# A look-ahead of three steps instead of six for the row maxima of a causal attention

## The reference

```python
h = layernorm(x) * (1 + ca) + sa
q = h @ wq            # 32 heads of 8
k, v = h @ wk, h @ wv # 8 heads of 8, each shared by 4 query heads
att = q @ k.T / sqrt(8), causal mask
att = softmax(att)    # over 1024 keys
x = x + ga * ((att @ v) @ wo)
h = layernorm(x) * (1 + cb) + sb
x = x + gb * ffn(h)   # 16 experts, top 4, and a shared one
```

## Time and profile before

| | |
|---|---|
| median of 3 runs | 1020.0 us (1019.06 to 1022.02) |
| profiled execution: its own time, its span | 1020.0 us, 1018.3 us |
| attention stage: first unit to first score | 89.7 to 124.28 us |
| attention stage: first score to the last product's end | 124.28 to about 603.9 us |
| TensorE busy over the span | 936.2 us (92%) |
| VectorE, ScalarE, GpSimd busy | 696.2, 434.4, 203.1 us |

### The profile page before, as it was taken

The page is one execution under the profiler, slowest core; times in us unless marked ns, Lnnn a source line. Parts: engine busy times, 40 slices in busy tenths (PEclk is TensorE's granted clock), DMA queues, the critical chain, the costliest instruction groups (busy, mean ns, idle before and its releaser), DMA issues. The chain is left out here.

```text
span 1018.3 us, 15458 instructions
## 1 busy us (share of the span) xinstructions
PE 936.2 (92%) x5728; PEld 687.0 (67%) x5728; DVE 696.2 (68%) x1242; ACT 434.4 (43%) x624; POOL 203.1 (20%) x241
## 2 busy tenths in 40 slices
PE   2884999999999999999999977769999999999996
PEld 2643766666666666666666426757888888888885
DVE  6535978877778877778877315478666666665665
ACT  1010066666666656566656761412232232223221
POOL 9500022221111211111211212487000000000000
PEclk8695599999999999999999998579999999999998
DMA  5174003333112222112220015143000000000000
GB/s 171 57 149 139 18 14 72 70 61 56 35 36 57 54 46 56 34 37 56 52 48 16 23 60 158 31 124 95 1 13 8 0 0 21 0 0 21 0 0 21
DMA packets 40550, 48.60 MB, mean 48 GB/s; under 512 B 10000, under 2 KB 29456, under 8 KB 39952
## 3 DMA queue, kind: packets, MB, share of 16 engines
q1 hardware_dynamic: 40496, 47.88, 19.8%
HBM read 29.77 MB, written 17.56 MB: 46 GB/s over the span
## 5 line engine op out<-in xcount | busy, mean ns | idle before, releaser
L574 ACT ACTIVATE probs<-psum 128x1024 f32<-128x1024 f32 (+3 forms) x384 | 294.5, 812 | 204.1 <-PE psum L624 202.3
L675 DVE TENSOR_REDUCE max_parts<-psum 128x1 f32<-128x512 f32 (+2 forms) x384 | 257.0, 687 | 13.4 <-PE psum L611 7.6
L624 PE MATMUL psum<-qs,ks 128*128 128x512 f32 (+3 forms) x768 | 208.3, 355 | 1.1 <-ACT probs L574 0.6
L671 DVE TENSOR_REDUCE max_parts<-psum 128x1 f32<-128x512 f32 x192 | 132.5, 690 | 78.3 <-PE psum L598 75.6
L638 PE MATMUL psum<-probs,v_aug 128*32 128x512 f32 (+3 forms) x1536 | 163.4, 498 | 0.2 <-POOL probs L551 0.2
L948 ACT ACTIVATE mid<-psum 128x512 f32<-128x512 f32 x80 | 47.9, 599 | 243.4 <-PE psum L971 243.4
L624 PEld LDWEIGHTS psum<-qs,ks 128*128 128x128 f32 x768 | 131.1, 189 | 25.9 <-ACT probs L574 15.8
L551 POOL TENSOR_SCALAR_AFFINE_SELECT probs<-probs 128x512 f32<-128x512 f32 x128 | 81.4, 636 | 300.9 <-ACT probs L574 300.9
L608 PE MATMUL psum<-ks,qs 128*128 128x256 f32 (+3 forms) x448 | 134.7, 335 | 0.0
L1059 DVE TENSOR_TENSOR mid<-mid,psum 128x512 f32<-128x512 f32 x80 | 54.9, 687 | 104.0 <-ACT mid L948 103.4
L611 PE MATMUL psum<-kd,qs 128*128 128x128 f32 x512 | 101.3, 267 | 18.3 <-DVE ks L691 18.3
(11 more groups left out here) (127 smaller groups left out, 1002.9 us busy)
## 6 DMA issues: line engine op xcount, KB each, us to landing
qs<-q_parts SPq DMA_DIRECT2D x32, 256.0 KB
y_sums<-y_sb SPq DMA_DIRECT2D x32, 256.0 KB, 2.3
wl_raw<-in_L_ffn_we_dram SPq DMA_DIRECT2D x36, 128.0 KB, 2.3
x_sb<-in_L_attn_x_dram SPq DMA_DIRECT2D x4, 512.0 KB, 7.2
q_parts<-w_hi SPq DMA_DIRECT2D x8, 256.0 KB
k_parts<-k_parts_sb SPq DMA_DIRECT2D x16, 128.0 KB
q_parts<-w_lo SPq DMA_DIRECT2D x8, 256.0 KB
ks<-k_parts SPq DMA_DIRECT2D x16, 128.0 KB
```

The costliest lines, as they stand in the source:

```text
L574: act.activation(probs[:, s % (LAG + 1), 2 * hh:2 * hh + 2, off:TT], psum[:, 2 * hh:2 * hh + 2, off:TT], ACT.Exp, scale=SCALE).then_inc(p_ ...
L624: last = pe.matmul(bank[2 * hh + hp][:, off:TT], ks[buf][:, c * P:(c + 1) * P], qs[buf][:, 2 * hh + hp, half * TT + off:(half + 1) * TT], ...
L671: dve.tensor_reduce(out=max_parts[:, hh, hp, i:i + 1, 1], in_=bank[unit_bank[u % 3]][:], axis=AX.X, op=ALU.max).then_inc(unit_free, 1)
L675: dve.tensor_reduce(out=max_parts[:, h0:h1, kind, slice(*tiles), slot], in_=bank[unit_bank[u % 3]].rearrange("p (s w) -> p s w", w=w), axi ...
```

## The change

The look-ahead becomes three triples, and the place of `split_rows` on GpSimd moves from behind s7's to behind s9's mask, because the last triple of the next group now falls in s8 instead of s5. TensorE, VectorE and SyncE take their new order from the constant; no instruction is added or removed over the whole kernel.

```diff
-AHEAD = 6
+AHEAD = 3
...
-                        if s == NSTEP - AHEAD + 1 and group + 1 < GROUPS:
+                        if s == NSTEP - AHEAD and group + 1 < GROUPS:
                             split_rows(group + 1)
```

## The result

The changed kernel takes 1075.62 us (median of 4, 1073.38 to 1081.94), the kernel before 1021.01 us (median of 4). The ratio is 1.0545, 95% interval 1.0495 to 1.0595. The direction was right and the size wrong: +13 us was forecast, up to +22 in the range, and +55 us came. The span grew from 1018.3 to 1075.2 us, by 56.9.

A forecast was written before the change was run, and what follows sets the result against it. TensorE was taken to bound the attention stage, so added waits cost one for one. Start -4.4, moved units +2.2, boundary waits +12.0 and last boundary +3.2 gave +13.0 us on 1020.0: 1033 us, range 1020 to 1042.

The forecast's parts named there:

- The start: Attention stage's first score: at 119.9 instead of 124.28 us, gaining 4.4 us; up to 1.5 us of low clock allowed.
- The moved units and the stream: Nine units moved into s6 to s8 of group 14 cost 2.2 us; a group's TensorE stream stays 30.73 us.
- the stream would get shorter: Rival, 8%: heavy triples beside the shortest scores shorten each group by over 0.87 us; at 1.1 us, 1016.5 us total.
- The chain to the read: Group boundary, from s9's first score (t9): cast at t9 + 3.0, first write t9 + 3.57, read issued t9 + 6.40.
- The slow chains: Writes-to-read chains at 14 boundaries: five exceed 2.83 us, by 4.6 us together, passing through as waits.
- the forecast's own lower bound: Low end of the forecast's own bounds, 1024 to 1042 us, before the range took in most of the just-in-time case.
- Before group 15: Last boundary, where s9 to s11 have no units: TensorE waits 3.2 us (2.7 to 3.7).
- the landing of the read: Read of the rows of maxima: lands 2.0 us after issue (1.5 to 2.5), at t9 + 8.40, so TensorE waits 0.53 us.
- the score that was due later: Next group's first score at a boundary: due 7.87 us after s9's first score (t9).
- the falling clock: Rival, 8%: after a wait, above all before group 15, TensorE falls to 1.2 GHz, costing 5 to 6 us; 1039 total.
- the rows come just in time: Rival, 14%: read lands in 1.5 us, writes no slower than 2.83, no wait at 14 boundaries; 1020 us, within 0.3%.
- the forecast's mechanism: Main case, 70%: TensorE waits for the rows of maxima at each group boundary; 1025 to 1042 us.

The follow-up runs named there:

- e2: Changed kernel with GpSimd's split of the rows behind s8's mask instead of s9's: 1036.41 us, ratio 1.0145 to the kernel before.
- e1: Changed kernel with SyncE sending the five loads of load_stacks after the sums of the group before, not right behind the rows' read: 1049.71 us, ratio 1.0288.
- e3: Changed kernel with eight extra overwritten matmuls of 512 columns ahead of the wait for the rows, from group 1 on: 1058.83 us, ratio 1.0375.
- e9: Kernel before with the split behind s9's mask and eight overwritten matmuls ahead of the wait for the rows: 1073.83 us, ratio 1.0524.
- e4: Kernel before, look-ahead of six kept, with only the split moved behind s9's mask: 1090.48 us, ratio 1.0685.

## Why the prediction was wrong

**The start: right.** First score at 120.24 (forecast 119.9), after a wait of 1.16 us (0.6). The clock rose 2.9 us behind it, at 123.1, instead of 0.9 us behind it, at 125.2; that costs about a us, within the 1.5 allowed.

**The moved units and the stream: right.** The nine units cost 2.3 us (2.2). A group of the same order without a wait takes 30.71 us (e2, 280.26 to 310.97; 30.73 before), so the new places of the heavy triples cost or save nothing. The rival that the stream would get shorter is refuted.

**The chain to the read: right.** Mask, split and writes came within 0.2 us of the forecast. The slow chains were there too: four of the 14, 4.2 us longer together than 2.83 each (4.6 reckoned). The mean of the 16 chains before is 3.12 us and not the 3.04 written down, and the forecast's own lower bound comes out at 1023 and not 1024; neither enters the sum. Before group 15 the wait was 4.5 us (3.2), by a slow chain of 3.47 us and a read of 2.73.

**The term that was mis-sized: the landing of the read.** I took 2.0 us, between the writes' 1.5 and the sums' 2.3, with 2.5 as the upper bound. It measured 3.72 with the loads behind it and 2.7 without. I had even written down that the loads of `load_stacks` stand behind `rows_in` on SyncE, and asked only whether they come too late. I did not ask what they do to the transfer ahead of them. Before, the two were more than nine us apart; the new order sets one 0.3 us behind the other (290.15 and 290.44). At 13 boundaries 1.72 us more is 22.4 us, and the three other reads were 0.5 to 0.7 us slower than taken; against that stand 14 x 0.18 = 2.5 us for the shorter chain and 14 x 0.14 = 2.0 for the score that was due later (by modelled ends; from start to start, in e2, it is due at t9 + 7.84). That is the 20 us by which the waits came out longer. The Trainium skill's formula (DMA: Bandwidth & Descriptors, Anatomy of one DMA) would have given 2.1 us, an estimate from that page, and was no nearer. The same page of the Trainium skill (Latency and other measured facts) says that this fixed part shrinks when the memory is less loaded; e1 fits that, 3.72 against 2.71 us, but the loads of expert weights, which load it too, slowed the read much less (mean 2.9), and no run here tells load of the memory from other effects of the five loads.

**The step that was missing: the clock.** I had the falling clock as a rival with a chance of 8% and a price of 6 us, and argued that one wait in 30 us leaves TensorE busy for 98% of it. That average was the mistake. The clock fell at 11 of the 14 waits from group 0 to group 14, which were 1.6 to 3.9 us long, each time for 3.4 or 6.8 us, and once more before group 15. With 1.5 us a fall or more it came to 20 us. e3 and e9 show the link by taking the idle time away at an unchanged order of the work. When a wait brings a fall and when not stays open: in the changed kernel waits of 0.92, 1.26 and 1.52 us had none and those from 1.58 us on had, but in e3 and e9 waits of 2.63 and 2.46 us, right behind the filler, had none. Nor does the length alone decide without the filler: one wait of e4 was 2.94 us, the clock stood at 1.00 when it began, and it stayed there for the next 32.7 us.

```profile
228.84 0.73 PE L624 MATMUL psum<-qs,ks 128*128 128x512 f32 x2 [2.94 <-DMA qs<-max_rows]
...
228.84:261.54 32.70, 30.98 (x216) 19.86 (x216) 24.36 (x38) 20.09 (x27) 7.33 (x11) 1.00 0.30 54
```

**The rivals.** That the rows come just in time was the case I gave 14%. It needs a read of 1.5 us, which none of the runs shows. That the waits bring the clock down was the true one, together with the forecast's mechanism, and I had priced it once instead of at each boundary.

**The slow write chains.** The prediction took their number from the kernel before and gave no cause. The sums' DMA, which it named as a possible neighbour, isn't it: in the changed kernel it is issued 11 us ahead of the writes (375.30 and 386.64 at group 8), and that chain takes 4.03 us all the same. The traces show another neighbour. This is the DMA view of that chain (386.64 to 390.67), with the median landing of the four writes:

```profile
q8 instruction: 1, 0.02, 2.0%
...
max_rows<-neg_parts SPq DMA_DIRECT2D x4, 8.0 KB, 2.1
```

The next chain, 2.82 us long, has no such row, and its writes land in 1.5 us. The eleven traces have 176 chains. 46 take 2.9 us or more, up to 4.99, and in each of them a transfer of a queue that the profile calls instruction (q8 or q14) is under way between the first write and the read. Of the 130 that take 2.80 to 2.85 us, 112 have none and 18 have one. The places fit as well: e1 and e2 have their slow chains at the changed kernel's groups (1, 8, 12, 14 and 15; e2 a weak one at 11 besides), kernels with another look-ahead or with the filler have some of them elsewhere, and e4 has one only, before group 15. This link is read from traces alone. No experiment here moved these transfers, so it is not shown that they are the cause.

## What to carry to other kernels

A look-ahead is not only slack in time. It also keeps transfers apart, so ask of a shortened one which transfers it sets side by side, and give a transfer that an engine waits for the price of the busy case, unless a row shows that these neighbours leave it alone. When work is handed on through an in-order queue, put it at the place where its input is ready, not at the place that the loop's arithmetic gives: here the same look-ahead costs 15 us or 55 us by the place of the split. And a wait on a TensorE that is otherwise full costs more than its length, as the clock may fall behind it, so a short wait that comes back often has to be priced with a fall each time.

## What was not expected of the hardware

- A read of 32 KB in two long runs released TensorE 2.4 to 3.0 us after its issue when nothing followed it for 7 us. With the five loads of `load_stacks` issued 0.3 us behind it on the same queue it was 3.05 to 4.09 us in the changed kernel. With three loads of expert weights there instead it was 2.52 to 3.38 us, in nine reads of all runs.
- A chain of four small writes and the wait for them took 2.80 to 2.85 us in 130 of 176 cases and up to 4.99 us in the others, and all of these had a transfer of an instruction queue in them.
- TensorE's clock fell to 1.2 GHz behind single waits of 1.6 to 2 us, though the engine had been busy without a break for more than 30 us before, and at several boundaries was at work again when the clock fell. It came back 3.4 or 6.8 us later, with the work unchanged. A wait of 2.94 us (e4) brought no fall.
- Eight matmuls of 512 columns in the place of the wait, 1.8 us at full clock, kept it up at every boundary of e3, and at all but two of e9.
